# Attention with heads stacked two to a block of rows, fp32 projections, PSUM shared as one ring per reader, and the rotary sines on GpSimd

## What is computed

```python
x = x + attention(layernorm(x), ctx)      # per batch: 8 heads of 16 channels
#   q, k, v = W @ input + b;  q, k turned by rotary angles
#   scores = q.k / 4 over 512 x 512;  softmax;  average of v;  output projection
x = x + experts(layernorm(x))             # 2048 tokens, top 8 of 32 experts
```

## Time and profile before

| | us |
|---|---|
| median of 3 runs | 1250.21 (1248.09 to 1252.45) |
| the profiled execution | 1247.21 |
| its span | 1245.4 |
| PE busy | 1077.0 (86%) |
| DVE busy | 774.4 (62%) |
| ACT busy | 772.5 (62%) |
| POOL busy | 754.8 (61%) |

### The profile page before, as it was taken

How to read it: one execution, slowest core, us unless ns; L and a number is a source line. 1 busy time by engine, 2 the same in 40 slices (tenths; PEclk the granted TensorE clock), 3 DMA queues, 4 the chain that set the end, 5 groups by cost and what they waited for, 6 DMA issues and landing times.

```text
span 1245.4 us, 31224 instructions
## 1 busy us (share of the span) xinstructions
PE 1077.0 (86%) x7188; PEld 519.6 (42%) x7189; DVE 774.4 (62%) x1514; ACT 772.5 (62%) x1520; POOL 754.8 (61%) x628
## 2 busy tenths in 40 slices
PE   2499989899999999985079989999999989999997
PEld 0123333333333333321046555655565555555564
DVE  4677989898989999864734544445444544354421
ACT  2177777777777777774146655766566655566664
POOL 5223365565555566535747657766776666677776
PEclk9999999999999999998579989999999999999999
DMA  4223334333333333431068888898898888888883
GB/s 135 89 79 100 100 88 106 97 97 90 101 98 101 104 88 80 130 97 45 20 178 177 205 201 168 204 210 210 196 194 205 210 188 179 207 194 188 169 149 65
DMA packets 142649, 172.53 MB, mean 139 GB/s; under 512 B 76259, under 2 KB 97123, under 8 KB 138373
## 3 DMA queue, kind: packets, MB, share of 16 engines
q0 software_dynamic: 38896, 76.67, 30.2%
q1 hardware_dynamic: 103700, 95.26, 27.0%
q10 hardware_dynamic: 2, 0.02, 0.0%
HBM read 119.20 MB, written 58.81 MB: 143 GB/s over the span
## 4 chain that ended last, share of the span: by engine, by line
PE 22%; DMA 15%; issue 14%; DVE 8%; POOL 7%; ACT 3%; DVEq 2%; POOLq 0%; SPq 0%; ACTq 0%
DMA pr<-normalised_tokens,g_idx 12%; PE ps L1241 10%; POOL expert_rows L527 4%; PE ps L1249 3%; DVE w_lo L1066 3%; DMA out<-v,s_idx 2%; DVE w_hi L1062 2%; POOL o_n L575 1%; PE ps L1271 1%; PE ps L1270 1%; PE ps L1269 1%; PE ps L1268 1%; PE ps L1267 1%; DVE mx L814 1%; ACT o_raw L644 1%
## 5 line engine op out<-in xcount | busy, mean ns | idle before, releaser
L653 ACT ACTIVATE pr<-ps 128x512 f32<-128x512 f32 x512 | 289.4, 596 | 107.8 <-PE ps L1191 105.7
L814 DVE TENSOR_REDUCE mx<-ps 128x2 f32<-128x1024 f32 x256 | 307.1, 1212 | 57.5 <-PE ps L1214 52.0
L1241 PE MATMUL ps<-w_hi,o_raw 128*128 x1232 | 329.7, 330 | 0.0
L628 POOL DMA_INDIRECT out<-v,s_idx x152 | 258.3, 1699 | 114.1 <-issue 72.3
L1214 PE MATMUL ps<-k_st,q_st 128*128 128x512 f16 x512 | 195.2, 386 | 35.6 <-DVE mx L814 21.5
L1191 PE MATMUL ps<-q_st,k_st 128*128 128x512 f16 x512 | 194.9, 382 | 25.9 <-ACT pr L653 23.0
L612 POOL DMA_INDIRECT pr<-normalised_tokens,g_idx x158 | 166.1, 1052 | 79.8 <-issue 36.1
L1241 PE MATMUL ps<-w_lo,o_raw 128*128 x616 | 203.0, 330 | 0.0
L644 ACT ACTIVATE o_raw<-ps 128x1024 f16<-128x1024 f16 (+1 forms) x187 | 177.5, 949 | 34.4 <-PE ps L1249 25.1
L1076 DVE SCALAR_TENSOR_TENSOR rope_b<-rope_a,s_idx,ps 128x192 f32<-128x192 f32 x153 | 63.2, 413 | 172.9 <-ACT rope_a L733 90.2
L1241 PEld LDWEIGHTS ps<-w_hi,o_raw 128*128 128x128 f16 x1232 | 122.0, 99 | 91.1 <-issue 6.1
(11 more groups left out here) (158 smaller groups left out, 1474.2 us busy)
## 6 DMA issues: line engine op xcount, KB each, us to landing
stage<-in_expert_w SPq DMA_DIRECT2D x32, 1280.0 KB
w_lo<-in_x SPq DMA_DIRECT2D x32, 256.0 KB, 3.6
qk_parts<-qk SPq DMA_DIRECT2D x16, 512.0 KB, 3.0
rcb<-reciprocals SPq DMA_DIRECT2D x128, 64.0 KB, 2.1
q_st<-qk_parts SPq DMA_DIRECT2D x96, 64.0 KB
k_st<-qk_parts SPq DMA_DIRECT2D x96, 64.0 KB
w_lo<-in_ctx SPq DMA_DIRECT2D x16, 256.0 KB, 3.3
out<-x SPq DMA_DIRECT2D x16, 256.0 KB, 4.1
```

What stands on the lines that cost most here:

```text
L628: nc.gpsimd.indirect_dma_start(out_rows, bass.IndirectOffsetOnAxis(s_idx[:, s.slot(GROUP), 1:2], 0), y_sb[:, s.slot(4), :], None, bounds_c ...
L653: nc.scalar.activation(pr[:, n % 8, :], ps_s[n % 2], ACT.Exp, scale=DH ** -0.5).then_inc(exp_done, 1)
L814: V.tensor_reduce(mx[:, b.slot(2), k, 2 * h:2 * h + 2], ps_m[h], AXX, ALU.max).then_inc(mx_done, 1)
L1241: last = mm(ps[:, s.slot(2), 0:2 * INTER], xt[:, s.slot(2), at:at + P], w[:, cols], start=(m == 0), stop=(m == 3 * KT - 1))
```

## The change

- **Stacks.** Heads h and h+4 now share a block: one stack in rows 0-47, the other in rows 64-111, the row of the maximum at 48 and 112. `q_st` and `k_st` hold 4 pairs instead of 8 heads. A pair of scores is two matmuls of 49 (maxima: 48) rows, each on its own half of the rows and into its own bank. A half of a stack is now twelve transfers of 16 rows by 2 heads; the constant row is loaded once at the start, and no rows are cleared. The mrow store is two transfers.
- **Projections.** q, turned q, k, turned k and v are each one fp32 product (v: four of 128 columns) of `xn` or `c_in`. The fp16 parts of x and ctx, and the operations that made them, are gone.
- **PSUM.** Two pairs of banks form a ring whose reader is mostly DVE (maxima, q and k jointly, logits, counts, output); three banks form a ring whose reader is ACT (scores, turned q, turned k, v, transposes); one bank is the averages'. A job waits for the reader of the job that had its bank last (`bank_is_free`).
- **Rotary step.** DVE applies the cosine to q and k. ACT reads turned q and turned k with their bias (`turned_half`), POOL multiplies by the sine (`rope_sin`) and adds. POOL also computes `shift`, which DVE did.
- **Orders.** The slots of the smaller jobs, DVE's and POOL's order, and SP's order are new.

The diff, cut to its core:

```diff
-SHARE = 2 * DH + DH
+SHARE = 3 * DH
+SIDE = P // 2
...
-        ps_m = [ps[:, 0:2, :], ps[:, 2:4, :]]
-        ps_s = [ps[:, 4, :], ps[:, 5, :]]
-        ps_o = ps[:, 6, :]
-        ps_x = ps[:, 7, :]
-        ps_xh = ps_x.bitcast(F16)
+        v_bank = [ps[:, 0:2, :], ps[:, 2:4, :]]
+        s_bank = [ps[:, 4 + n, :] for n in range(3)]
+        ps_o = ps[:, 7, :]
...
+        def in_v_banks(it):
+
+            b1, bp, bo, br = it + 1, it + 2, it + -1, it + -2
+            best = [(f"m{n}", b1, mx_done, b1.count(16, n + 1)) for n in range(16)]
+            return (best[0:2] + [("qk", bp, rope_done, bp.count(2, 2))] + best[2:10] + [("lg", br, lg_done, br.count(1, 1))] +
+                    best[10:14] + [("cnt", br, cnt_done, br.count(2, 2))] + best[14:16] + [("y", bo, x2_done, bo.count(1, 1))])
+
+        def in_s_banks(it):
+
+            b2, b1, bp, br = it, it + 1, it + 2, it + -2
+            e = [(f"s{n}", b2, exp_done, b2.count(32, n + 1)) for n in range(32)]
+            return (e[0:6] + [("mt1", b2, mrow_done, b2.count(2, 2))] + e[6:8] + [("qr", bp, turned, bp.count(2, 1))] +
+                    e[8:10] + [("kr", bp, turned, bp.count(2, 2))] + e[10:12] + [("v", b1, v_done, b1.count(1, 1))] +
+                    e[12:14] + [("xt", br, xt_read, br.count(1, 1))] + e[14:22] + [("mt0", b1, mrow_done, b1.count(2, 1))] + e[22:32] + [None])
...
+                    order, ring = tenants_of(it + -1) + now, len(banks)
+                    at = len(now) + names.index(name)
+                    assert len(now) % ring == 0
+                    for place in range(at - ring, -1, -ring):
+                        if order[place] and order[place][1].live():
+                            need(eng, *order[place][2:])
+                            return
...
+                if b1.live():
+                    load_stack(b1, 1)
...
+                if bl.live():
+                    need(sp, v_mm, bl.count(1, -1))
+                    sp.dma_start(c_in[:, bl.slot(2), :], of(ctx, bl)).then_inc(c_loaded[bl.slot(2)], 16)
...
+                if bp.live():
+
+                    sp.wait_ge(qk_lo, bp.count(2, 2))
+                    sp.dma_start(of(q_stack_d, bp).rearrange("a p t -> p a t"), qk[:, :, :]).then_inc(qk_stored, 16)
                 if b2.live():
                     den_store(b2, 0)
                 if bp.live():
-
-                    sp.wait_ge(qk_lo, bp.count(2, 2))
-                    sp.dma_start(of(q_stack_d, bp).rearrange("a p t -> p a t"), qk[:, :, :]).then_inc(qk_stored, 16)
+                    sp.wait_ge(qk_stored, bp.count(16, 16))
+                    apart(sp)
+                    load_stack(bp, 0)
+                if b1.live():
+                    store_mrow(b1, 0)
                 if b2.live():
                     den_load(b2, 0)
-                if b1.live():
-                    store_mrow(b1, 0)
-                if bp.live():
-                    sp.wait_ge(qk_stored, bp.count(16, 16))
-                    load_stack(bp, 0)
                 if b2.live():
                     rcp_round(b2, 0)
...
             def load_stack(b, half):
 
                 need(sp, s2_mm, b.count(32, -64 + 16 * (half + 1)))
-                if isinstance(b.k, int) and b.count(1) < 2 and half == 0:
-                    sp.wait_ge(q_clear, 1)
-                    sp.wait_ge(k_clear, 1)
-                heads = slice(4 * half, 4 * half + 4)
-
-                sp.dma_start(q_st[SHARE:SHARE + 1, b.slot(2), heads, :], const_m[0:1, 0:4 * T].rearrange("o (h t) -> o h t", h=4)).then_inc(stack_in[b.slot(2)][half], 16)
+                apart(sp)
+                two = slice(2 * half, 2 * half + 2)
                 for st, parts in ((q_st, (0, 0, 1)), (k_st, (2, 3, 2))):
-                    for r, part in enumerate(parts):
-                        src = of(q_stack_d, b)[part].rearrange("(h c) t -> c h t", c=DH)[:, heads, :]
-                        sp.dma_start(st[DH * r:DH * (r + 1), b.slot(2), heads, :], src).then_inc(stack_in[b.slot(2)][half], 16)
+                    for g in range(2):
+                        heads = slice(4 * g + 2 * half, 4 * g + 2 * half + 2)
+                        for r, part in enumerate(parts):
+                            src = of(q_stack_d, b)[part].rearrange("(h c) t -> c h t", c=DH)[:, heads, :]
+                            at = SIDE * g + DH * r
+                            sp.dma_start(st[at:at + DH, b.slot(2), two, :], src).then_inc(stack_in[b.slot(2)][half], 16)
 
             def store_mrow(b, half):
                 sp.wait_ge(mrow_done, b.count(2, half + 1))
-                sp.dma_start(q_st[SHARE:SHARE + 1, b.slot(2), 4 * half:4 * half + 4, :].rearrange("p h (j t) -> p (h j) t", j=NSC),
-                             mrow[:, half, :]).then_inc(mrow_in[b.slot(2)][half], 16)
+                for g in range(2):
+                    at = SIDE * g + SHARE
+                    sp.dma_start(q_st[at:at + 1, b.slot(2), 2 * half:2 * half + 2, :].rearrange("p h (j t) -> p (h j) t", j=NSC),
+                                 mrow[8 * g:8 * g + 8, half, :]).then_inc(mrow_in[b.slot(2)][half], 16)
...
                     scale_o(bo, 0)
+                scatter_rows(bs, (0, 1))
                 if br.live():
                     gp.wait_ge(x2_hi, br.count(1, 1))
                     need(gp, tok_stored[br.slot(2)], br.rounds(2, 16, 0))
                     sub(x2s[:, br.slot(2), LO, :], xn2[:, :], x2s[:, br.slot(2), HI, :]).then_inc(x2_lo, 1)
-                scatter_rows(bs, (0,))
                 if bp.live():
+                    rope_sin(bp, 0)
                     rope_add(bp, 0)
-                scatter_rows(bs, (1,))
+                    rope_sin(bp, 1)
+                    rope_add(bp, 1)
                 if bl.live():
                     gp.wait_ge(stat1, bl.count(3, 3))
                     need(gp, xn_done, bl.count(1))
-                    nc.gpsimd.tensor_tensor(rstd[:, 0:1], vare[:, 0:1], cf[:, HALF:HALF + 1], ALU.pow).then_inc(rstd1, 1)
-                scatter_rows(bs, (2,))
+                    normalising(0, rstd1, shift1, bl)
                 if bp.live():
                     low_of_qk(bp, 0)
-                if bp.live():
-                    rope_add(bp, 1)
+                scatter_rows(bs, (2,))
                 if bp.live():
                     low_of_qk(bp, 1)
                 if bo.live():
                     scale_o(bo, 1)
-                scatter_rows(bs, (3,))
-                scatter_rows(bs, (4,))
-                if bl.live():
-
-                    gp.wait_ge(xc_hi, bl.count(2, 1))
-                    need(gp, proj_mm, bl.count(4, -4))
-                    sub(xs[:, bl.slot(2), LO, :], xn[:, :], xs[:, bl.slot(2), HI, :])
-                    gp.wait_ge(xc_hi, bl.count(2, 2))
-                    need(gp, v_mm, bl.count(1, -1))
-                    sub(cs[:, bl.slot(2), LO, :], c_in[:, bl.slot(2), :], cs[:, bl.slot(2), HI, :]).then_inc(xc_lo, 1)
-                scatter_rows(bs, (5, 6, 7))
+                scatter_rows(bs, (3, 4, 5, 6, 7))
+
+            def normalising(norm, rstd_done, shift_done, b):
+                nc.gpsimd.tensor_tensor(rstd[:, norm:norm + 1], vare[:, norm:norm + 1], cf[:, HALF:HALF + 1], ALU.pow).then_inc(rstd_done, 1)
+                gp.wait_ge(rstd_done, b.count(1, 1))
+                apart(gp)
+                nc.gpsimd.tensor_scalar(shift[:, norm:norm + 1], mv[:, norm, 0:1], rstd[:, norm:norm + 1], -1.0, ALU.mult, ALU.mult).then_inc(shift_done, 1)
+
+            def rope_sin(b, w):
+                gp.wait_ge(turned, b.count(2, w + 1))
+                nc.gpsimd.tensor_tensor(rope_b[:, w, :], rope_b[:, w, :], cf[:, SIN:SIN + T], ALU.mult).then_inc(turned_sin, 1)
...
+            def turned_half(b, w):
+                act.wait_ge(turn_mm, b.count(2, w + 1))
+                need(act, rope_sum, b.count(2, w - 1))
+                nc.scalar.activation(rope_b[:, w, :], bank("kr" if w else "qr"), ACT.Identity, bias=pb[:, 2 * w + 1:2 * w + 2]).then_inc(turned, 1)
...
+                others = {(1, 0): (bo, lambda: read_o(bo, 1)), (1, 2): (b2, lambda: max_row(b2, 1)), (1, 3): (br, high_of_x2),
+                          (2, 0): (bp, lambda: turned_half(bp, 0)), (2, 2): (bp, lambda: turned_half(bp, 1)), (3, 0): (b1, lambda: read_v(b1)),
+                          (3, 1): (bp, lambda: high_of_qk(bp, 0)), (3, 2): (br, read_xt), (4, 0): (bp, lambda: high_of_qk(bp, 1)),
+                          (5, 0): (b2, lambda: read_o(b2, 0)), (5, 2): (b1, lambda: max_row(b1, 0)), (5, 3): (br, exponentials_of_top),
+                          (6, 2): (bl, normal_x)}
...
+                maxima(0)
+                if bp.live():
+                    rope(bp, 0)
+                    rope(bp, 1)
+                if isinstance(it.k, int) and it.count(1) == NB + 1:
+                    first_weights()
+                maxima(1)
+                maximum(b1, 4)
+                if bl.live():
+                    dve.wait_ge(x_loaded[bl.slot(2)], bl.rounds(2, 16, 16))
```

(50 more changed lines are left out.)

266 lines of the change are left out of this document (99 added, 167 removed).

## The result

| | before | after |
|---|---|---|
| median (range) | 1251.3 us (1248.1 to 1252.6) | 1414.6 us (1399.9 to 1421.6) |
| profiled execution, its span | 1247.2, 1245.4 | 1399.9, 1398.1 |
| mean granted clock | 0.966 | 0.902 |
| a turn, of fourteen | 32.6 us | 42.6 us |

The ratio is 1.127, 95% interval [1.118, 1.136]: slower, as forecast (1339), but by 163 us in place of 88, and outside the range of 1250 to 1385. The profiled execution is the fastest of the four; the slowest, 1421.6, lies over 1.5% above it and is left out of the ratio.

A forecast was written before the change was run, and what follows sets the result against it. VectorE was taken to bound a turn before the change; after it, 21.4 + 12.2 + 6.5 = 40.1 us, taken as 39.2, is 6.6 over 32.6, times fourteen 92 us, less 3 outside: 1336 profiled, 1339 median, range 1250 to 1385.

The forecast's parts named there:

- The order of SyncE's queue: Denominators' load now behind stack and mrow transfers: VectorE waits 3 to 8 us ahead of the first-half reciprocal each turn.
- Steps 1 to 3: Turn's start, through projections and scores, to ScalarE reading turned q: 11.0 us into the turn (10.0 if never late).
- Step 4: GpSimd's sines, sums, normalising, scatter and low parts: k's low part done at 21.4 us (bounds 19.7, 21.9).
- Step 5: SyncE, store of q and k to denominators landed, with twelve issues and mrow: 12.2 us (bounds 10.4 and 13.9).
- Step 6: From VectorE's reciprocal through maxima 13 and 14 and counts to the output projection: 7.2 us, less 0.75, 6.5.
- The walk: The path through one turn after the change, all steps summed: 40.1 us, bounds 36.5 and 43.0; 39.2 was taken.
- the case's own upper end: Top of the forecast case's own range, fourteen turns each 10.4 us longer: 1393 us; the case's chance was 0.63.
- Start and end: Outside the fourteen turns, a clear lost, transfer issues gained, last two turns' waits lost: -3 us (between -10 and +6).
- Outside the profiled run: Whole kernel: the median of the runs was taken as 3 us above the profiled execution, 1339 over 1336.
- the first: Rival: paired 64-row matmuls on TensorE run one after the other, 41 us a turn, 1365 us; chance 0.08.
- the second: Rival: SyncE issues the small transfers at 0.24 us each, 37 us a turn, 1309 us; chance 0.12.
- The faster one: Rival: denominators arrive before VectorE's reciprocal, 28.5 to 32 us a turn, say 30.5, total 1220 us; chance 0.12.

The follow-up runs named there:

- a1: The kernel after, with SyncE loading the first half's denominators ahead of the twelve stack transfers: 1334.1 us, ratio 1.065.
- b1: The kernel before, with the first half's denominators' load moved behind the stack's transfers and the mrow store: 1340.1 us, ratio 1.071.
- r1: The kernel after with the denominators' load in front, heads back on rows 0 to 48 of a block each, matmuls on all 128 rows: 1316.3 us, ratio 1.048.
- b2: The kernel before, with the two shift operations computed by GpSimd and not by VectorE: 1240.4 us, ratio 0.989.
- a2: The kernel after, with 24 idle matmuls a turn on 48 rows added on TensorE ahead of score 28: 1440 us, ratio 1.151.
- a4: The kernel after, with 32 idle matmuls a turn of 384 columns on all 128 rows ahead of score 28: 1445 us, ratio 1.141.
- b7: The kernel before, with score matmuls on rows 0 to 48 and maxima matmuls on rows 0 to 47, not all 128: 1322 us, ratio 1.050.

## Why the prediction was right in kind and wrong in size

- **The order of SyncE's queue** was the decisive step, and right. The gap ahead of the first-half reciprocal is 5.0 us (3 to 8 said), the twelve issues are 0.48 apart, VectorE's share is 61 to 63% (70% said). a1 and b1 show the price: 80 to 88 us, where 92 less 3 was forecast for the whole change. That the two are so near is chance: the 92 count from before's 32.6 us a turn, the 80 from a1's 37.6, which the prediction did not foresee, and both measured prices hold half clock, which it did not foresee either.
- **Steps 1 to 3**: turned q read at 11.4 us (11.0), turned k at 14.1 (13).
- **Step 4**: k's low part done at 23.0 (21.4; upper bound 21.9). GpSimd's first sine starts 0.8 us behind ScalarE's reading, its fourth operation ends at 17.6 (16.1), and the high half of k came at 21.1 (20.2). 1.6 us short.
- **Step 5**: 12.6 us (12.2).
- **Step 6**: 8.3 us (6.5), the step that failed: it priced TensorE's work behind the wait at full clock. The 0.75 us for `rows<-ex,exr` did go: 0.23 us now, with GpSimd idle beside it. The two more products on GpSimd held nothing up where it can be seen: VectorE's statistics beside the first sine took 0.68 us (418.33), as in before. But in this turn the average took 0.9 and the output projection 1.6 us more, at half clock; over thirteen turns the output projection took 0.95 more. That with a wait of 5 us TensorE would run some 10 us a turn at half clock stood in no step and no bound. b1 shows that it happens with full rows too.
- **The sum.** The walk gave 40.1, this turn took 43.9, the mean of fourteen was 42.6. I had taken 39.2 "since the lower bound assumes only that engines are on time"; that was a discount with no row behind it, and cost 0.9 x 14 = 13 us. The rest, 2.5 x 14 = 35 us, I put down to the clock and step 4, by this one turn; how it divides over fourteen is not shown. The mean turn lies within the walk's own bounds (36.5 to 43.0). What took the time past even 1393, the case's own upper end, were the two terms that follow.
- **Start and end**: +12 us, not -3. Up to the first scores, 3.7 us later, the clock was 0.73; that this made them late is not shown. Behind the fourteen turns it is 8.2 us: the fourteenth output projection comes 36.2 us behind the thirteenth, where before needs 29.8. The waits lost in the last two turns were a gain that did not come.
- **Outside the profiled run**: the median of after lies 15 us above its profiled execution; I had taken 3.
- **The rivals.** Pairs overlap, so the first fell. Small transfers issue no faster, so the second fell. The faster one asked for the denominators in time. a1 made them so, and was still 6.5% slower: a turn of 37.6 and not 28.5 to 32 (its own terms give 28.2 to 31.2). It allowed 2 to 5 us for signals and for waiting on fp32 projections; in r1 VectorE waits 7.5 us a turn for maxima matmuls alone. It had nothing for few rows (1.7% in this order, 4 to 5% alone in the old one) and for the clustered jobs. Of the parts of the change that I costed at nothing or a gain and that were run alone, only the shifts gained (b2).
- **Two readings.** The 2.2 us a turn that VectorE waits for maxima matmuls in before are most of its 3.6 us without work, and not little of it. And a price for a change of mode was in before's trace: the 0.31 from a score to an average.

The parts alone add to 7.1 (order) + 4.1 (stacks) + 2.6 (fp32) = 13.8%, the whole is 12.7%. That is no account of it: the parts overlap, two of them were measured with the pause, and the rings were never run alone. How much of the 4.8% of r1 is rings and how much fp32 stays open.

## What to carry to other kernels

Follow the queue that issues the transfers, in order: one small load moved behind a burst of transfers cost 80 to 88 us, half of what the change did, and splitting transfers in two doubles the time to issue them. A wait on an otherwise busy TensorE can be dearer than its length: with 5 us of it a turn, half clock took 5.4 us (b1) to 10 us (after) of each turn, so price the rows behind such a wait at half clock too. Taking zero rows out of a matmul saves nothing in itself (0.38 to 0.39 us for either), and only the move of a few small operations off the bounding engine (b2) paid.

## What the runs showed of the hardware

- TensorE's clock fell to 1.2 GHz while matmuls on 48 rows ran back to back (a2), held at 2.4 through matmuls on 128 rows in the same place of the program (a4), and stayed low for 103 us of all but unbroken work mostly on 48 rows at the start of b7. In b7's ten later turns it held at 2.4 on the same rows.
- A wait of 5 us a turn alone brought 65 us at half clock in twelve turns of full rows (b1), where before has none.
- Two matmuls on rows 0 to 48 and 64 to 112 overlap wholly: 0.39 us for both.
- A change from 48-row to 128-row matmuls adds 0.09 us (0.31 against 0.22 from start to start, 88 steps in b7); so does one from 128 columns to 32 in before.
- SyncE takes 0.48 us to issue a transfer of 32 KB as of 64 KB with many short pieces.
- A window's clock can read 1.00 where the trace has no record of it; lengths of like matmuls tell.
- Chips differ: on three of five, SyncE, ScalarE and VectorE lose 2 to 3 us once a turn, and the same kernel before takes 1 to 2% longer.
